# Value products moved from the projection into the first head's maximum pass, and the projection's order rewritten

## The reference

```python
Q = (x @ Wq + bq).reshape(B, S, Hn, Dh)
K = (x @ Wk + bk).reshape(B, S, Hn, Dh)
V = (x @ Wv + bv).reshape(B, S, Hn, Dh)
attn = softmax(where(causal, einsum(Q, K) * scale, -inf))
h = x @ dp_w1 + dp_b1                       # "drift", 128 wide
h = (h - mu) / jnp.sqrt(var + LN_EPS) * ln_g + ln_b
drift = (_gelu(h) @ dp_w2 + dp_b2)[..., 0]
g = _gelu(drift[..., None] * g_w1[0] + g_b1)
gate = jnp.tanh(g @ g_w2 + g_b2)[..., 0]
out = einsum(attn * gate, V) @ Wo + bo
```

## Time and profile before

| | us |
|---|---|
| three runs | 2906.12, 2900.37, 2904.73 |
| profiled execution, its own time | 2903.9 |
| its span | 2902.1 |
| PE / DVE / ACT / POOL busy | 2623.9 / 2257.8 / 1626.8 / 199.5 |

### The profile page before, as it was taken

The page is one execution under the profiler, slowest core; times in us unless marked ns, Lnnn a source line. Parts: engine busy times, 40 slices in busy tenths (PEclk is TensorE's granted clock), DMA queues, the critical chain, the costliest instruction groups (busy, mean ns, idle before and its releaser), DMA issues. The chain is left out here.

```text
span 2902.1 us, 86251 instructions
## 1 busy us (share of the span) xinstructions
PE 2623.9 (90%) x36424; PEld 1590.9 (55%) x36424; DVE 2257.8 (78%) x4398; ACT 1626.8 (56%) x2406; POOL 199.5 (7%) x228
## 2 busy tenths in 40 slices
PE   6889999999999999999999998999988999218996
PEld 3332556656666655666566634555545666116774
DVE  3559899999999999999899824565556998675877
ACT  2320677777777777777777791111116777215663
POOL 1238000000000000000000000000000000100000
PEclk8995899999999999999999999999998999559998
DMA  4234011011110111101110001000000333314442
GB/s 144 88 97 83 3 28 29 5 27 28 28 28 5 27 28 28 28 6 27 28 29 7 4 21 52 16 28 15 15 8 27 91 104 94 117 33 109 120 120 64
DMA packets 158654, 133.32 MB, mean 46 GB/s; under 512 B 103097, under 2 KB 135995, under 8 KB 153275
## 3 DMA queue, kind: packets, MB, share of 16 engines
q1 hardware_dynamic: 152571, 124.08, 17.8%
q10 hardware_dynamic: 4224, 4.19, 0.5%
q0 software_dynamic: 1536, 0.40, 0.1%
HBM read 79.98 MB, written 46.66 MB: 44 GB/s over the span
## 5 line engine op out<-in xcount | busy, mean ns | idle before, releaser
L709 DVE TENSOR_REDUCE attn_pm<-attn_MS 128x1 f32<-128x512 f32 (+3 forms) x2304 | 1331.2, 638 | 114.6 <-PE attn_MS L753 97.0
L695 ACT ACTIVATE attn_PT<-attn_ES 128x1024 f32<-128x1024 f32 (+5 forms) x1152 | 1040.8, 951 | 389.7 <-PE attn_ES L788 385.8
L803 PE MATMUL attn_OP<-attn_PT,attn_VH 128*17 128x512 f32 (+2 forms) x4608 | 641.8, 558 | 0.4 <-issue 0.2
L753 PE MATMUL attn_MS<-head_KX,head_QX 96*32 96x512 bf16 (+12 forms) x3456 | 395.5, 393 | 4.3 <-DVE attn_pm L709 3.5
L753 PE MATMUL attn_MS<-attn_KX,attn_QX 96*32 96x512 bf16 (+9 forms) x2880 | 316.0, 365 | 2.0 <-DVE attn_pm L709 1.1
L753 PE MATMUL attn_MS<-after_attention,attn_QX 96*32 96x512 bf16 (+7 forms) x2880 | 314.9, 358 | 1.5 <-DVE attn_pm L709 1.0
L788 PE MATMUL attn_ES<-head_QX,head_KX 99*32 99x512 bf16 (+5 forms) x3456 | 283.1, 360 | 7.0 <-ACT attn_PT L695 4.4
L788 PE MATMUL attn_ES<-attn_QX,after_attention 99*32 99x512 bf16 (+10 forms) x2880 | 243.1, 358 | 1.9 <-DMA attn_QX<-attn_parts 1.6
L788 PE MATMUL attn_ES<-attn_QX,attn_KX 99*32 99x512 bf16 (+8 forms) x2880 | 239.7, 357 | 0.0
L1189 PE MATMUL l0out_ring<-l0out_w,l0out_sT 128*128 128x512 f32 x512 | 224.9, 592 | 0.0
L753 PEld LDWEIGHTS attn_MS<-head_KX,head_QX 96*32 96x32 bf16 x3456 | 144.8, 97 | 131.7 <-DVE attn_pm L709 62.5
(11 more groups left out here) (295 smaller groups left out, 3345.0 us busy)
## 6 DMA issues: line engine op xcount, KB each, us to landing
vk_beta<-front_vk SPq DMA_DIRECT2D x8, 1024.0 KB, 4.0
kq_transposed<-l0out_w_in SPq DMA_DIRECT2D x8, 1024.0 KB, 4.4
delta_VK<-vk_beta SPq DMA_DIRECT2D x32, 256.0 KB, 2.8
delta_QK<-kq_transposed SPq DMA_DIRECT2D x32, 256.0 KB, 2.9
attn_QX<-qk_parts SPq DMA_DIRECT2D x60, 128.0 KB, 7.4
after_attention<-attn_out SPq DMA_DIRECT2D x18, 256.0 KB
x_res<-in_L_attn_x_dram ACTq DMA_DIRECT2D x8, 512.0 KB, 7.8
qk_parts<-project_hi SPq DMA_DIRECT2D x8, 512.0 KB, 2.9
```

The lines of the kernel that those rows point to most:

```text
L695: nc.scalar.activation(PT[u % NPT][:, 512 - wa:512 + wb], ES[half][:, 512 - wa:512 + wb], ACT.Exp, scale=DH ** -0.5).then_inc(exp_done, 1)
L709: nc.vector.tensor_reduce(pm[r][:, i, c:c + 1], MS[slot][:, 0:w], AX.X, ALU.max).then_inc(max_taken, 1)
L753: last = nc.tensor.matmul(MS[slot][r, 0:seen], QX[b][0:ROWS, i * P + 32 * g:i * P + 32 * g + 32], KX[b][0:ROWS, 512 * c:512 * c + seen], s ...
L803: last = nc.tensor.matmul(OP[32 * j:32 * j + DH + 1, 512 - w:512], VH[b][:, kt, :], PT[(2 * n + half) % NPT][:, o:o + w], start=(kt == 0), ...
```

## The change

- `hT` gets a buffer for each of the eight groups. They lie in memory that is not used yet: the four `PT` buffers, `QX2` (queries of head 2) and `after_attention` (keys of head 2).
- The value products leave `project`. There is one function `values(t)` per tile of 128 tokens in the maximum pass of head 0: after piece 3 + 7t // 2 PE makes the tile's 256 columns from `hT` into the exp stage's score banks (`ES`), and ACT copies each pair of tiles to `v17` (`take_values`). The gate's three steps on ACT stand between these copies, and POOL's last gate step waits for the last pair. The load of head 2, and all loads behind it on SP, wait for it too.
- In `project` PE's drift tiles have only their 128 columns. Q and K have four PSUM banks, `hi` and `mid` two buffers each, `r1` two instead of four, and `lo` one as before.
- The order in `project` is new: PE transposes group g + 1 behind the first product of g, DVE normalises two groups ahead and the drift one group behind, ACT takes up `hi`, `mid`, `hT` and the square roots in a new order. Loops over groups are written out.
- The row of ones for head 2's keys is set by POOL after its first `split_max`.

```diff
-    V = Steps("r1_0", "r1_1", "r1_2", "r1_3", "v", "haggr", "hrstd", "hn")
-    A = Steps("hi_0", "mid_0", "hi_1", "mid_1", "hi_2", "mid_2", "hi_3", "mid_3", "hstd")
-    M = Steps("qk_0", "qk_1", "qk_2", "qk_3", "vh_0", "vh_1", "vh_2", "vh_3")
+    V = Steps("r1_0", "r1_1", "r1_2", "r1_3")
+    HV = Steps("hstats", "haggr", "hrstd", "hn", back=2)
+    A = Steps("hi_0", "hi_1", "mid_0", "hi_2", "mid_1", "hi_3", "mid_2", "mid_3")
+    HA = Steps("hstd")
+    M = Steps("qk_0", "qk_1", "qk_2", "qk_3", "drift")
...
-        hi = sb("hi", [P, 4, 512], BF16); mid = sb("mid", [P, 4, 512], BF16); lo = sb("lo", [P, 4, 512], BF16)
-        r1 = sb("r1", [P, 4, 512])
+        hi = [sb(f"hi{b}", [P, 4, 512], BF16) for b in range(2)]
+        mid = [sb(f"mid{b}", [P, 4, 512], BF16) for b in range(2)]
+        lo = sb("lo", [P, 4, 512], BF16)
+        r1 = sb("r1", [P, 2, 512])
...
-        tp = ps("tp", [P, EH, 512]); qkp = ps("qkp", [P, 2, 512]); vhp = ps("vhp", [P, 4, 512])
+        tp = ps("tp", [P, EH, 512]); qkp = ps("qkp", [P, 4, 512]); hp = ps("hp", [P, 2, J, HID])
...
+            for g in range(G):                      # ACT
+                first_part(g, 0)
+                if g + 1 < G:
+                    modulate(g + 1)
+                first_part(g, 1)
+                second_part(g, 0)
+                if g + 2 < G:
+                    spread(g + 2)
+                first_part(g, 2)
+                second_part(g, 1)
+                first_part(g, 3)
+                if g >= 1:
+                    drift_spread(g - 1)
+                second_part(g, 2)
+                second_part(g, 3)
...
+            for g in range(G):                      # POOL
+                for m in range(4):
                     pool.wait_ge(ad, A(g, f"mid_{m}"))
-                    pool.wait_ge(lo_out, LO * g + 16)
-                    nc.gpsimd.tensor_tensor(lo[:, m, :], r1[:, m, :], mid[:, m, :], ALU.subtract).then_inc(pd, 1)
+                    if g >= 1:
+                        pool.wait_ge(lo_out, LO * g)
+                    nc.gpsimd.tensor_tensor(lo[:, m, :], r1[:, m % 2, :], mid[g % 2][:, m, :],
+                                            ALU.subtract).then_inc(pd, 1)
...
+            for g in range(G):                      # DVE
+                rest(g, 0)
+                if g >= 1:
+                    drift_statistics(g - 1)
+                rest(g, 1)
+                if g + 2 < G:
+                    statistics(g + 2)
+                rest(g, 2)
+                if g + 2 < G:
+                    normalise(g + 2)
+                rest(g, 3)
+                if g >= 1:
+                    drift_normalise(g - 1)
...
+            for g in range(G):                      # PE
+                product(g, 0)
+                if g + 1 < G:
+                    turn_over(g + 1)
+                for m in range(1, 4):
+                    product(g, m)
+                drift(g)
...
+        pool.wait_ge(values_taken, pairs)           # Gate.on_pool, before the last step
...
+        PAIRS = T // 2
+        values_at = {3 + 7 * t // 2: t for t in range(T)}
...
-            for b in range(1, NB):
-                load(b, b)
+            load(1, 1)
+            sp.wait_ge(v_taken, PAIRS)
+            load(2, 2)
...
+            def take_values(v):
+                act.wait_ge(v_made, v + 1)
+                nc.scalar.activation(v17[:, 2 * v:2 * v + 2, :, 0:DH],
+                                     ES[v // 2 % 2][:, v % 2 * 512:v % 2 * 512 + 512]
+                                     .rearrange("p (t h c) -> p t h c", t=2, c=DH), ACT.Copy).then_inc(v_taken, 1)
+            for v in range(PAIRS):
+                take_values(v)
+                if v == 5:
+                    gate.hidden_on_act(act)
+                if v == 11:
+                    gate.wide_on_act(act)
+                if v == 13:
+                    gate.gate_on_act(act)
...
+            def values(t):
+                v, g, j = t // 2, t // J, t % J
+                if v >= 4 and t % 2 == 0:
+                    pe.wait_ge(v_taken, v - 3)
+                o = v % 2 * 512 + t % 2 * E
+                dst = ES[v // 2 % 2][:, o:o + E]
+                nc.tensor.matmul(dst, k["ones"][0:1, :], bvh[:, 0:E], start=True, stop=False)
+                for h in range(EH):
+                    last = nc.tensor.matmul(dst, hT[g][:, h, j * P:(j + 1) * P], wvh[:, h, 0:E],
+                                            start=False, stop=(h == 1))
+                if t % 2:
+                    last.then_inc(v_made, 1)
...
                 max_piece(0, n % 3, n)
+                if n in values_at:
+                    values(values_at[n])
```

More of the change, by code:

```diff
@@ L225, in _ @@
         def _(sp):
-            for out in (hi_out, mid_out, lo_out):
-                sp.sem_inc(out, 16)
             sp.dma_start(head.mask[:], d["c_mask"].rearrange("a p n -> p a n")).then_inc(head.mask_in, 16)
             gate.load(sp)
-            with sp.Fori(0, G) as g:
+            for g in range(G):
+                b = g % 2
                 cols = bass.ds(g * 512, 512)
@@ L261, in modulate, with first_part @@
                 for h in range(EH):
-                    last = nc.scalar.activation(hT[:, h, :], tp[:, h, :], ACT.Identity,
+                    last = nc.scalar.activation(hT[g][:, h, :], tp[:, h, :], ACT.Identity,
                                                 bias=k["mod0"][:, h:h + 1], scale=k["mod0"][:, 2 + h:3 + h])
                 last.then_inc(fad, 1)
[L266 to L278, removed]
+            def first_part(g, m):
+                act.wait_ge(md, M(g, f"qk_{m}"))
+                if g >= 2:
+                    act.wait_ge(hi_out[g % 2], HI * (g // 2))
+                nc.scalar.activation(hi[g % 2][:, m, :], qkp[:, m, :], ACT.Identity, bias=bqk[:, m:m + 1])\
+                    .then_inc(ad, 1)
@@ L281, in _ @@
             act.sem_inc(fad, FA.primed)
+            act.sem_inc(had, HA.primed)
             spread(0)
             modulate(0)
[L284 to L287, removed]
+            spread(1)
+            for g in range(G):
[13 more added lines that the diff above has]
+                second_part(g, 3)
@@ L352, in _ @@
             dve.sem_inc(vd, V.primed)
+            dve.sem_inc(hvd, HV.primed)
+            statistics(0)
             normalise(0)
-            for g in range(0, G - 1):
-                for m in range(2):
-                    rest(g, m)
-                normalise(g + 1)
-                for m in range(2, 4):
-                    rest(g, m)
-                values(g)
-            for m in range(4):
-                rest(G - 1, m)
-            values(G - 1)
+            statistics(1)
+            normalise(1)
+            for g in range(G):
[11 more added lines that the diff above has]
+                    drift_normalise(g - 1)
+            drift_statistics(G - 1)
+            drift_normalise(G - 1)
         @block.tensor
@@ L396, in _ @@
             turn_over(0)
-            with pe.Fori(0, G - 1) as g:
-                products(g)
-                turn_over(g + 1)
-            products(G - 1)
+            for g in range(G):
+                product(g, 0)
[4 more added lines that the diff above has]
+                drift(g)
 KPARTS = (0, 0, 0, 1, 1, 2)
@@ L565, in attention @@
         KX = [head.KX, sb("KX1", [P, S], BF16), after_attention[:].bitcast(BF16)]
[L566 removed]
+        QX = [head.QX, sb("QX1", [P, S], BF16), QX2]
         VH = [sb(f"VH{b}", [P, T, DH + 1]) for b in range(NB)]
[L568 removed]
         OS = [sb("OS0", [P, 512]), last_rows]
@@ L631, in _ @@
         def _(pool):
-            for b in range(NB):
+            for b in range(2):
                 nc.gpsimd.memset(KX[b][ROWS:MAXR, :], 1.0).then_inc(ready, 1)
@@ L661, in _ @@
                 split_max(h, h % NB, entry_count(h + 1, TURN_AT) + 1)
+                if h == 0:
+                    nc.gpsimd.memset(KX[2][ROWS:MAXR, :], 1.0).then_inc(ready, 1)
+                    pool.wait_ge(ready, NB + 1)
             split_max(H - 1, (H - 1) % NB, entry_count(H, 0) + 1)
```

133 lines of the change are left out of this document (77 added, 56 removed).

## The result

| | before | after |
|---|---|---|
| median of nine runs each, us | 2902.44 (2898.81 to 2908.24) | 2881.89 (2865.49 to 2891.22) |
| ratio, 95% interval | 1 | 0.9925 (0.9902 to 0.9948) |
| profiled execution, and its span | 2903.9, 2902.1 | 2891.22, 2889.4 |
| first piece of the maximum pass | 210.0 | 152.92 |
| DVE's nm reduction, which closes the pass | 290.4 | 279.33 |

The change makes the kernel 20.6 us faster; 2877 was forecast. The spans of the two profiled executions differ by 12.7 us, and 11.1 of that lie ahead of the exp stage; the last row differs by 1.6. The profiled execution is the slowest of the nine, so its trace shows more loss than the median has.

What follows compares the result with a forecast made beforehand. No engine was full in the projection; DVE bound the maximum pass. Span: 2902.1 - 54.6 (projection) + 27 (pass) = 2874.5; on the median 2904.7 - 27.6 = 2877 us, range 2862 to 2890.

Steps and rivals of the forecast that it cites:

- The projection's turn: Projection: turns of 20.9 us become two at 12.1 and five at 12.9; pass starts 54.6 us earlier.
- The loop through the landing of lo: Projection: lo of group g+1 waits for lo of g to land; 25.9 us for two turns, 12.9 for one.
- The tile in the pass: Maximum pass: a value tile of six 256-column records takes 1.7 us at full clock, bounds 1.3 and 1.9.
- The rounds: Maximum pass: a tile with three pieces takes 2.35 us, with four 2.97, mean 2.66; pass 107 against 80.4.
- The clock: Maximum pass: PE starts at 0.50, costing some 3 us, then runs at full level through the value stretch.
- rival 1: Clock stays at 0.50 throughout the pass: tile 2.95 us, round 4.45, pass +82, time 2932; chance 0.15.
- Rival 2: Clock level goes to and fro in the pass: 2890 to 2915, about 2900; chance 0.10.
- my case: Whole kernel: main forecast of 2877 us with its own range of 2862 to 2890; chance 0.55.
- What lay beside it: Around the pass: GpSimd's gate chain, ACT's copies and head 2's loads cost 0, with up to 5 us above.
- Rival 5: Projection: weight loads don't overlap 128-column products; PE's turn 15.1 us, 18 more in all, 2895; chance 0.02.
- Rival 4: Projection: SyncE's queue and the landings set the turn, near 15 us: 2894; chance 0.08.
- rival 3: Maximum pass: PE's slack takes in the tiles, DVE stays fed; pass +5, 2855; chance 0.10.

Runs made afterwards that it cites:

- e4_lo2: e1_warm with lo in two buffers instead of one (one r1 buffer moved to free memory): 2870.25 us, ratio 0.9891.
- e1_warm: Changed kernel plus twelve extra PE products, results unread, filling the pause between projection and maximum pass: 2873.68 us, ratio 0.9896.
- e2_in_projection: Changed kernel's new projection order, but value products stay in the projection and the maximum pass has none: 2876.7 us, ratio 0.9911.
- e3_no_bias: Changed kernel without the one-row bias products in the value tiles, pause not filled: 2849.78 us, ratio 0.9817.
- e5_full_rows: Changed kernel with the values' bias product made from all 128 rows, zeros below the first, pause not filled: 2870.96 us, ratio 0.9883.
- e6_split: e1_warm with each value tile's three products placed one by one behind 96 pieces: 2880.68 us, ratio 0.9935.
- e7_all: Changed kernel with e5_full_rows (drift tiles too), e1_warm, e4_lo2 and e6_split edits together: 2875.94 us, ratio 0.9909.

## Why the prediction was right

**The projection's turn.** Predicted: two turns at 12.1, five at 12.9, PE's own work at 12.1. Measured from drift to drift: 12.0, 12.3, 12.6, 13.7, 12.6, 13.1, a mean of 12.7 (the last, without transposes, 11.1); PE's own turn 11.96 in e4_lo2. From the first products, at 41.23, to those of the last group, at 132.19, it is 91.0 us where 91.2 was forecast. Drift, 1.06 us a tile, came out to the hundredth, out of the earlier trace rows. The loop through the landing of lo is there, from the second turn on; two buffers took it away. DVE's round of its list in it was put at 8.8 us of work and is 9.35, because normalising a tile takes 0.62 us instead of 0.41. The first piece at 152.92 against 155.4: 57.1 gained where 54.6 was forecast. Most of the 2.5 us is the tail, 20.7 us from the last group's products to the first piece, taken to be 22.6 as before.

**The tile in the pass.** 1.7 us predicted, 1.68 measured from its first record to the next piece, and 1.80 with the 0.12 that lie ahead of it. The prediction took two changes of 0.19, both laid to the one row, and kept a third, between pieces and whole rows, for its upper bound of 1.9. The runs show three: 0.12 into the whole array, 0.19 from one row to 128, 0.19 back to pieces. The term was 0.1 us too small.

**The rounds.** 2.35 and 2.97 predicted for three and four pieces, 2.42 and 3.21 measured in e1_warm; the means, 2.66 and 2.75, differ by 0.09 us, near the 0.12 us ahead of the tile. Where the pass starts at full clock it is 106.8 us, 26.4 more than the old one. In the projection the values cost 33.0 us (first piece at 185.94 in e2_in_projection, at 152.92 in the changed kernel), so with the clock up the move would be worth 7 us, and in the profiled execution, at 46.0 us for the pass, it lost 13.

**The clock, where the step failed.** "I take the full level for the value stretch", with 3 us for the start. In the profiled execution the start at 0.50 lasted 47 us and cost 19.6, not 3. At that level rival 1 is right in its numbers: 2.95 us for a tile and 4.45 a round against 3.15 and 4.6 measured. It was wrong that it lasts: the clock rose at 200. Rival 2, a level that changes within the pass, at 2890 to 2915, describes this execution (2891.22); the median of nine runs lies between it and my case. That it lies within 5 us of 2877 is in part luck: what the forecast left out, a low stretch at the start of the pass, cost 16.6 us more than forecast where it was traced, and the nine executions, in which its length seems to differ, are spread from 2865.49 to 2891.22. The argument for the full level was the absence of waits, by analogy with the starts of the projection turns and of the exp stage. Those stretches have no waits, but they have no one-row products, or few; by e3_no_bias and e5_full_rows that is the likely difference. The fact against it stood in the prediction, under rival 1, as "a third of each tile's columns has only one row". The Trainium skill ("TensorE: Matmul & The Clock Gate", Part 1, What's actually happening) has the level follow how busy PE has been; by the trace PE was busy for 40.00 of 40 us at 0.50, so busy time as the profile counts it does not decide alone.

**What lay beside it.** The gate's last step ran from 261.38 to 275.25, 4 us ahead of nm; from nm to the scores it is 10.3 us, as before; the loads of head 2 cost nothing. All three were put at 0.

**Rival 5** is refuted by the drift tile: with loads that do not overlap it would be 1.8 us and not 1.06. The rule of the Trainium skill that stood beside it ("TensorE: Matmul & The Clock Gate", Part 3, The mechanism) gives the 1.8, and the trace disagrees. The same section also lets a load run ahead into a background weight buffer; that case does not contradict the trace. **Rival 4** is out with turns under 14; **rival 3** too, since DVE idles 11.5 us between 210 and 255 at full clock.

## What to carry to other kernels

Work moved into a stage in which its engine "has room" has to be priced as a round of the receiving loop, with its buffers and its changes of array shape: the 33.0 us that the values cost in the projection came back as 26.4 us of pass at full clock and 46.0 in the profiled execution, and leaving them in place was worth as much. A bias as a one-row product costs more than its columns: filling the rows with zeros saved 1.5 us a turn in one kernel and, in the profiled executions, 23 us of pass in another, for one memset. About 6 of the 23 are the changes saved (106.8 against 100.7 us, with the pause filled in both); the rest is the clock's. And look at what sets the clock at the start of a stage: here the level behind a pause was worth 19.6 us in the one execution that was traced, and it is the likely source of the changed kernel's scatter of 26 us.

## What the runs showed of the hardware

- Behind a pause, a stretch with one-row products in it stayed at a granted 0.50 for 47 us with PE busy throughout; with the rows filled with zeros, or the products left out, it was at 1.00 within 10 us. A stretch that began at 1.00 kept it in spite of them (e1_warm). One trace of each kernel shows this; why it is so stays open.
- A change between one-row and 128-row products costs 0.19 us at full clock, to the hundredth in a projection turn (17.15 - 15.61 for eight of them), and 0.20 in a drift tile (1.06 - 0.66 for two).
- A change between 32-column pieces and whole-array products costs 0.12 us one way and 0.19 the other, however many rows the bias product has (the cycle of 0.95 us is the same in e6_split and e7_all).
- Filling a pause of 9.5 us with twelve products kept the clock at 1.00 and put the first piece 1.7 us later (e1_warm).
